# A language-model tower with a routed expert layer on one core: resident experts counted at once, engine orders written anew, and a broadcast product over 128 rows

## The chip, the cores and the metric

The kernel runs on one core of one Trainium2 chip. A core has five engines with a list of instructions each: PE (TensorE, matrix products), DVE (VectorE), ACT (ScalarE), POOL (GpSimd) and SP (SyncE, which here only issues transfers). They meet through semaphores alone. The metric is the device time of one execution in microseconds, as a median of runs.

## The reference

2048 tokens (16 tiles of 128) of width 256 go through two layers. The order of the sums is what matters here:

```python
h = _L0_tok_ref(x, L0_tok_weight)                       # gather of embedding rows
h = h + _L0_attn_ref(_layernorm(h), ...)                # causal linear attention, tile by tile (128 tokens)
h = h + _L0_ffn_ref(_layernorm(h), ...)                 # 256 x 256, scaled weights
h = h + _L1_attn_ref(_layernorm(h), ...)                # random-feature attention, 2-layer FFN
h = h + _L1_ffn_ref(_layernorm(h), ...)                 # router, 8 experts, shared expert

# in _L1_attn_ref, for the keys: the largest feature of a head over all tokens of the sequence
stab = jnp.max(xp, axis=(-1, -2), keepdims=True)
# in _L1_ffn_ref
logits = jnp.einsum('td,ed->te', x, router_w)
top_idx = jnp.argmax(logits, axis=-1)                   # one expert of 8 per token
score = jax.nn.sigmoid(jnp.max(logits, axis=-1))
g = jnp.einsum('td,edf->etf', x * score[:, None], expert_gate)
u = jnp.einsum('td,edf->etf', x * score[:, None], expert_up)
moe_out = jnp.einsum('te,etd->td', onehot, jnp.einsum('etf,efd->etd', silu(g) * u, expert_down))
return moe_out + silu(x @ shared_gate) * (x @ shared_up) @ shared_down
```

## The kernel before

**The token part.** Each of the 16 tiles goes through some 33 stages on PE and as many again on DVE, ACT and POOL: `a_...` is layer 0, `b_...` the attention of layer 1, `c_...` its FFN, the router and the shared expert. The order on an engine is a table of pairs (lag, stage) given to `run_steps`: in step u it runs, in the table's order, each stage for tile u - lag. So several tiles are under way, and the table alone decides what stands behind what. PSUM has 8 banks, which stages share; where two stages of different tiles use one bank, an `after(engine, name, count)` keeps them apart.

Stages that are named below: `b_kq` computes features of keys and queries, `b_km`, `b_kmT`, `kmx`, `b_kmB` find the largest key feature of a head (reduce on DVE, transpose on PE, reduce, and a product with a matrix of ones that gives it to all partitions), `b_qs` subtracts the queries' maxima. `c_T6`, `c_lo`, `c_log`, `c_choose` are the router; `c_cn` is the product that counts a tile's tokens by expert ("count"), `c_slot` turns it into rows of a sorted list, and POOL's `scat` scatters the tokens' numbers there (`sorted_ids`, in DRAM). `c_ga`, `c_up`, `c_dn` are the shared expert's gate, up and down on PE, `c_gc`, `c_hid` (writes `hT`) and `c_down` its parts on DVE. `x_out` and `home_out` on SP store a tile's scaled input and its sum so far to DRAM.

**The tables.** After the last tile's slots DVE computes from the counts which tiles of 128 sorted tokens belong to which expert: `table0` to `table3` for up to 16 whole tiles ("W"), `half_tables` for up to 8 halves of 64 tokens, two to a tile ("H"). `tile_row` and `half_row` give where a tile's ids start in `sorted_ids`; `tile_need` gives how many increments of `experts_ready` a tile's expert needs: max(1, expert - 2).

**The expert part.** 20 tiles in 10 rounds of two (WW, WW, WW, WH, WW, WH, ...; `yA` and `yB` hold the two inputs). POOL fetches their rows of x and of `home` by ids; PE transposes, computes gate and up (`yTA`, `yTB` with `we`), DVE and ACT the gating, PE down (`qkA`, `qkB`), DVE adds `home`, POOL stores to the output. Experts 0 to 3 ("resident", 1.5 MB each) are loaded at the start. Experts 4 to 7 ("late") take the place of the token part's weights, and the H tiles' experts that of `H_S`.

**SP's list at the end** is, in this order: the ids of groups 0 to 3 and the last stores of tiles by `run_steps`; late experts 4 and 5; ids of group 4; late experts 6 and 7; the two experts of the first H tile; ids of group 5; then

```python
            sp.wait_ge(S["residents_loaded"], 16 * RESIDENT)
            sp.sem_inc(S["experts_ready"], 1)
            for e in range(RESIDENT, E):
                sp.wait_ge(late_loaded[e], 16)
                sp.sem_inc(S["experts_ready"], 1)
```

PE waits for a whole tile's `need` of `experts_ready` up to round 5, and for all five later.

## Time and profile before

| | |
|---|---|
| median of 3 runs | 688.7 us (688.22 to 689.7) |
| the profiled execution, its own time | 687.8 us |
| its span, first to last instruction | 686.0 us (1.8 us lie around it) |
| mean granted TensorE clock | 0.973 |
| busy: PE, DVE, ACT, POOL | 619.5, 492.1, 285.8, 254.0 us |
| moved by DMA | 46.85 MB, 68 GB/s on the mean |

Busy shares are means over the whole span; what an engine waits for in one stretch is read from its timeline. A releaser behind an idle time is the instruction whose semaphore came last. A matmul of the code in float32 shows as two records in the trace.

### The profile page before, as it was taken

How to read it: one execution, taken by the hardware profiler on the slowest of the kernel's cores; microseconds unless marked ns; L12 is line 12 of the kernel's file. 1: busy time of each engine (PE TensorE's matmuls, PEld its weight loads, DVE VectorE, ACT ScalarE, POOL GpSimd, SP SyncE). 2: the span in 40 equal slices, each digit the busy share in tenths (PEclk: the TensorE clock that was granted, in tenths of full speed). 3: DMA queues.
4: the chain of work that ended last, by engine and by line, in shares of the span. 5: the costliest groups of instructions: out<-in, count | busy, mean ns of one | idle time of the engine just before them, and what ended most of it. 6: DMA issues, size and time to landing. Idle time of an engine off the chain costs nothing.

```text
span 686.0 us, 15421 instructions
## 1 busy us (share of the span) xinstructions
PE 619.5 (90%) x5960; PEld 500.2 (73%) x5960; DVE 492.1 (72%) x1171; ACT 285.8 (42%) x687; POOL 254.0 (37%) x405
## 2 busy tenths in 40 slices
PE   5878799998999999999999999999993079999997
PEld 4657588887888978898888988989992035555563
DVE  3998999999999988999989988976574012322322
ACT  2345566565465545546454454554320011222221
POOL 5443334435425342442524325312313014435433
PEclk9998999999999999999999999999998579999999
DMA  7950000000000000000000000000012861152550
GB/s 258 415 239 10 1 10 10 1 17 10 10 9 10 24 2 16 10 9 10 10 17 1 17 10 17 10 16 17 16 39 56 324 242 55 61 210 77 226 212 29
DMA packets 17367, 46.85 MB, mean 68 GB/s; under 512 B 6913, under 2 KB 11536, under 8 KB 14864
## 3 DMA queue, kind: packets, MB, share of 16 engines
q1 hardware_dynamic: 13136, 37.47, 14.4%
q0 software_dynamic: 4160, 8.41, 3.9%
q8 instruction: 48, 0.79, 0.7%
q14 instruction: 23, 0.19, 0.2%
HBM read 40.54 MB, written 6.89 MB: 69 GB/s over the span
## 4 chain that ended last, share of the span: by engine, by line
PE 65%; DVE 20%; issue 5%; ACT 3%; SPq 3%; DMA 2%; POOL 0%; another core or an unknown queue 0%; POOLq 0%; DVEq 0%; ACTq 0%
PE ps L1133 61%; DVE stats L716 3%; PE ps L1138 2%; DVE H_S L775 2%; DVE rdenTA L798 1%; SPq L318 1%; PE ps L1290 1%; SPq L317 1%; DVE qf L888 1%; DVE rdenTB L909 1%; ACT qkA L694 1%; DMA home_rows<-send_home 1%; DVE mv L717 1%; DVE x L732 1%; DVE H_S L732 1%
## 5 line engine op out<-in xcount | busy, mean ns | idle before, releaser
L415 POOL TENSOR_TENSOR var_eps<-mv,ln_eps 128x1 f32<-128x1 f32 x112 | 24.3, 217 | 280.2 <-DVE mv L717 275.4
L1133 PE MATMUL ps<-yTC,we 128*128 128x128 f32 x1024 | 123.1, 276 | 0.0
L1133 PEld LDWEIGHTS ps<-yTC,we 128*128 128x128 f32 x1024 | 120.0, 193 | 1.3 <-issue 0.2
L1133 PE MATMUL ps<-we,yTA 128*128 128x256 f32 (+1 forms) x272 | 89.3, 464 | 31.1 <-SPq L376 28.8
L1133 PEld LDWEIGHTS ps<-we,yTA 128*128 128x128 f32 x272 | 50.2, 198 | 52.9 <-issue 49.0
L416 POOL TENSOR_TENSOR rstd<-var_eps,pow_half 128x1 f32<-128x1 f32 x112 | 63.9, 570 | 8.8
L1133 PE MATMUL ps<-we,ffT 128*128 128x256 f32 x256 | 60.8, 380 | 0.0
L1133 PE MATMUL ps<-we,yTB 128*128 128x256 f32 (+1 forms) x176 | 54.8, 440 | 0.0
L1133 PEld LDWEIGHTS ps<-we,ffT 128*128 128x128 f32 x256 | 47.2, 190 | 6.9
L1133 PEld LDWEIGHTS ps<-we,yTB 128*128 128x128 f32 x176 | 32.2, 191 | 13.8 <-issue 11.5
L775 DVE TENSOR_TENSOR H_S<-ps,causal_sb 128x512 f32<-128x512 f32 x64 | 39.9, 677 | 2.0 <-PE ps L1133 2.0
L1114 DVE SCALAR_TENSOR_TENSOR kf<-kf,ps 128x512 f32<-128x512 f32 x10 | 6.9, 688 | 47.7 <-ACT kf L689 47.7
L689 ACT ACTIVATE kf<-ps 128x512 f32<-128x512 f32 x10 | 6.0, 597 | 80.2 <-PE ps L1133 80.2
L909 DVE RECIPROCAL rdenTB<-ps 128x256 f32<-128x256 f32 x16 | 28.1, 1753 | 9.4 <-PE ps L1133 9.4
L1133 PE MATMUL ps<-yTB,we 128*128 128x128 f32 x256 | 32.0, 278 | 2.4 <-ACT yTB L585 2.3
L1133 PEld LDWEIGHTS ps<-yTA,we 128*128 128x128 f32 x256 | 30.2, 192 | 4.4 <-issue 4.2
L1133 PE MATMUL ps<-yTA,we 128*128 128x128 f32 x256 | 32.3, 279 | 0.6 <-ACT yTA L554 0.6
L1133 PEld LDWEIGHTS ps<-yTB,we 128*128 128x128 f32 x256 | 29.8, 192 | 4.1 <-ACT yTB L585 3.5
L1133 PE MATMUL ps<-we,hT 128*128 128x256 f32 x128 | 31.3, 387 | 1.7 <-DVE hT L1082 1.6
L716 DVE BATCH_NORM_STATS2 stats<-H_S 128x6 f32<-128x256 f32 x64 | 27.2, 426 | 5.7 <-DMA H_S<-table,idx_sb 4.1
L625 ACT ACTIVATE kf<-kf 128x1024 f32<-128x1024 f32 x16 | 16.9, 1058 | 34.4 <-DVE kf L897 34.4
L513 POOL DMA_INDIRECT ffT<-home_rows,ids x20 | 20.5, 1024 | 28.7 <-DMA out<-tmpA,ids 15.7
(216 smaller groups left out, 1331.6 us busy)
## 6 DMA issues: line engine op xcount, KB each, us to landing
we<-w_experts SPq DMA_DIRECT2D x8, 1536.0 KB, 13.9
H_S<-w_experts SPq DMA_DIRECT2D x8, 1536.0 KB, 9.7
we<-w_ff SPq DMA_DIRECT2D x2, 1024.0 KB, 9.1
x_rows<-send_x SPq DMA_DIRECT2D x16, 128.0 KB, 1.7
home_rows<-send_home SPq DMA_DIRECT2D x16, 128.0 KB, 2.1
rows_sb<-rows SPq DMA_DIRECT2D x1, 1664.0 KB, 6.3
we<-w_qk SPq DMA_DIRECT2D x2, 512.0 KB, 4.5
we<-w_v SPq DMA_DIRECT2D x2, 256.0 KB, 4.7
```

The lines of the kernel that those rows point to most:

```text
L317: first = sp.value_load(table_of[0:1, k:k + 1], min_val=0, max_val=E * SPAN * P)
L415: link(pool.tensor_tensor(var_eps[:, k:k + 1], mv[:, k, 1:2], ln_eps[:], ALU.add))
L416: pool.tensor_tensor(rstd[:, k:k + 1], var_eps[:, k:k + 1], pow_half[:], ALU.pow).then_inc(S[f"rstd{k}_ready"], 1)
L513: pool.indirect_dma_start(out=home[s], out_offset=None, in_=home_rows, in_offset=by_id(j), bounds_check=T * P - 1, oob_is_err=False).then_ ...
L625: act.activation(flat(kf[:]), flat(kf[:]), ACT.Exp).then_inc(S["kexp_out"], 1)
L716: link(dve.bn_stats(stats[:, k], src))
L732: return dve.scalar_tensor_tensor(out=dst, in0=buf, scalar=rstd[:, k:k + 1], in1=rest, op0=ALU.mult, op1=ALU.add)
L775: dve.tensor_tensor(S_sb[:, b], by4(sc[b]), causal_sb[:].unsqueeze(1).broadcast_to([P, 4, P]), ALU.mult).then_inc(S["scores_masked"], 1)
L909: dve.reciprocal(rdenTB[:], nd1[:, D:2 * D]).then_inc(S["rden1_ready"], 1)
L1114: dve.scalar_tensor_tensor(out=eg2[s], in0=eg1[s], scalar=1.0, in1=banks_of[s][1], op0=ALU.add, op1=ALU.mult).then_inc(S["eg_ready"], 1)
L1133: return pe.matmul(o, a, b, start=start, stop=stop)
L1138: ins = pe.transpose(dst[:, c * P:(c + 1) * P], src[:, c * P:(c + 1) * P], id_sb[:])
```

## The change

Four things are changed, and no amount of work but for the broadcast.

1. SP's `ids0` increments `experts_ready` for the residents before it reads the first ids. The late experts are counted as soon as they are there: 4 and 5 ahead of the first halves' loads, 6 and 7 ahead of the ids of group 5.
2. The five tables of `run_steps` are new, and with them the PSUM banks of the stages and the `after` waits that they need. DVE's `b_norm` now waits for the `preB` of the tile before, and POOL's `pB` for `var4` of the tile before. On PE gate and up move from lags 9 and 10 to 11 and 11, down from 11 to 12.
3. SP reads ids of group 1 right behind group 0 and one store, group 2 and 3 behind the last stores.
4. `b_kmB` is a product with all 128 rows (`one_all`, `km_diag` of 128 partitions, of which 16 are written), where it had 16.

```diff
-        km_diag = sb("km_diag", [HEADS, HEADS])
-        one16 = sb("one16", [HEADS, P])
+        km_diag = sb("km_diag", [P, HEADS])
+        one_all = sb("one_all", [P, P])
...
                 if t == T - 1:
+                    sp.wait_ge(S["residents_loaded"], 16 * RESIDENT)
+                    sp.sem_inc(S["experts_ready"], 1)
                     sp.wait_ge(S["table_ready"], 1)
                     sp.wait_ge(S["ids_scattered"], 16 * T)
                     load_ids(0)
...
             run_steps([
-                (1, ids0), (10, ids3), (4, ids1), (0, x_out), (8, ids2), (2, home_out),
+                (1, ids0), (5, ids3), (0, x_out), (3, home_out), (1, ids1), (4, ids2),
             ])
...
+            def late_is_ready(e):
+                sp.wait_ge(late_loaded[e], 16)
+                sp.sem_inc(S["experts_ready"], 1)
+
             load_late(RESIDENT)
             load_late(RESIDENT + 1)
             load_ids(4)
             load_late(RESIDENT + 2)
             load_late(RESIDENT + 3)
...
+            late_is_ready(RESIDENT)
+            late_is_ready(RESIDENT + 1)
             sp.wait_ge(S["tile_done"], T)
             sp.wait_ge(S["table_ready"], 2)
             load_halves(0)
+            late_is_ready(RESIDENT + 2)
+            late_is_ready(RESIDENT + 3)
             load_ids(5)
-            sp.wait_ge(S["residents_loaded"], 16 * RESIDENT)
-            sp.sem_inc(S["experts_ready"], 1)
-            for e in range(RESIDENT, E):
-                sp.wait_ge(late_loaded[e], 16)
-                sp.sem_inc(S["experts_ready"], 1)
...
                 pool.wait_ge(S["src3_ready"], t + 1)
+                after(pool, "var4_ready", t)
                 pool.tensor_tensor(preB[:], yB[:], row["out1_bias"], ALU.add).then_inc(S["preB_ready"], 1)
...
             def b_norm(t):
-
+                after(dve, "preB_ready", t)
                 normalise(yB[:], H[:, t, :], 3, t).then_inc(S["src3_ready"], 1)
...
-                matmul(kb[:, 0:HEADS], one16[:], km_diag[:], True, True).then_inc(S["kmax_psum"], 1)
+                matmul(kb[:, 0:HEADS], one_all[:], km_diag[:], True, True).then_inc(S["kmax_psum"], 1)
...
-                (9, c_ga), (0, a_v), (7, c_lo), (5, c_T5), (1, a_num), (4, b_ctx),
+                (1, a_den), (4, b_v), (6, c_fa), (11, c_up), (5, b_out), (8, c_cn),
```

On PE, from the last tile's count to the first expert tile's transposes, there stood before (`yTC` of number k with `we` is gate or up of tile 12 + k, `hT` is down, `yA` the first expert tile's input):

```order
L1133 MATMUL ps<-onehot,ones_sb 128x8
L1133 MATMUL ps<-yTC_2,we 128x128 x8
L1133 MATMUL ps<-we,hT 128x256 x4
L1133 MATMUL ps<-yTC_2,we 128x128 x8
L1133 MATMUL ps<-yTC_3,we 128x128 x8
L1133 MATMUL ps<-we,hT 128x256 x4
L1133 MATMUL ps<-yTC_3,we 128x128 x8
L1133 MATMUL ps<-we,hT 128x256 x4
L1408 MATMUL ps<-id_sb,yA 128x128 x2
```

In the changed kernel the same stretch of PE's list reads:

```order
L1138 MATMUL ps<-onehot,ones_sb 128x8
L1138 MATMUL ps<-yTC_1,we 128x128 x8
L1138 MATMUL ps<-we,hT 128x256 x4
L1138 MATMUL ps<-yTC_1,we 128x128 x8
L1138 MATMUL ps<-yTC_2,we 128x128 x8
L1138 MATMUL ps<-we,hT 128x256 x4
L1138 MATMUL ps<-yTC_2,we 128x128 x8
L1138 MATMUL ps<-yTC_3,we 128x128 x8
L1138 MATMUL ps<-we,hT 128x256 x4
L1138 MATMUL ps<-yTC_3,we 128x128 x8
L1138 MATMUL ps<-we,hT 128x256 x4
L1418 MATMUL ps<-id_sb,yA 128x128 x2
```

Seven groups stood behind the last count, ten do now: one gate, one up and one down have moved behind it. On SP, at the reading of the first ids, this is the difference (`tile_row` loads an address, `ids` is the transfer, `home_rows` a tile's store):

```order
-L302 DMA x_rows<-send_x 128x256 [waits sent_ready]
+L317 TENSOR_LOAD tile_row [waits residents_loaded,table_ready,ids_scattered]
+L317 ISA x2
+L318 REGISTER_ALU
+L318 DMA ids<-sorted_ids 128x1
+L317 TENSOR_LOAD tile_row
+L317 ISA x2
+L318 REGISTER_ALU
+L318 DMA ids<-sorted_ids 128x1
 L307 DMA home_rows<-send_home 128x256 [waits tile_done]
```

The ids of group 0 now stand ahead of one more store of a tile, and the last three stores come behind them. Further down SP's list, behind the second pair of late experts, the changed kernel has:

```order
L351 DMA we<-w_experts 128x3072 x2
L361 TENSOR_LOAD half_expert [waits late_loaded4,late_loaded5,tile_done,table_ready]
L361 ISA x2
L362 ISA
L362 DMA H_S<-w_experts 128x3072
L361 TENSOR_LOAD half_expert
L361 ISA x2
L362 ISA
L362 DMA H_S<-w_experts 128x3072
L317 TENSOR_LOAD tile_row [waits late_loaded6,late_loaded7]
```

There the waits for the late experts now stand among the loads; before, they stood behind the ids of group 5.

## Rows read from the trace of the kernel before

**Rows 1.** The page's section 2, granted TensorE clock in 40 slices (tenths)

```profile
PEclk9998999999999999999999999999998579999999
```

**Rows 2.** Four stretches by windows; busy us of each engine, PEclk, DMA share, GB/s

```profile
0.00:506.40 506.40, 480.57 (x5368) 418.70 (x5369) 442.29 (x1058) 254.35 (x625) 192.25 (x344) 0.99 0.12 41
506.40:524.85 18.45, 13.99 (x95) 12.20 (x93) 12.12 (x45) 1.58 (x3) 3.02 (x3) 1.00 0.16 48
524.85:553.66 28.81, 0.00 (x1) 0.01 (x1) 1.79 (x9) 0.38 (x1) 3.99 (x4) 0.53 0.73 279
553.66:686.00 132.34, 124.97 (x500) 69.30 (x500) 35.94 (x60) 29.47 (x58) 54.77 (x54) 0.99 0.36 128
```

**Rows 3.** Timeline of PE, 500 to 554 us; start, duration, idle before and releaser

```profile
506.38 0.17 PE L1133 MATMUL ps<-onehot,ones_sb 128*128 128x8 f16 x1
...
519.23 1.99 PE L1133 MATMUL ps<-we,hT 128*128 128x256 f32 x8 [1.55 <-DVE hT L1082]
523.16 0.41 PE L1408 MATMUL ps<-id_sb,yA 128*128 128x128 f32 x2 [1.94 <-DMA yA<-x_rows,ids]
524.41 0.44 PE L1408 MATMUL ps<-id_sb,yB 128*128 128x128 f32 x2 [0.84 <-DMA yB<-x_rows,ids]
553.66 5.52 PE L1133 MATMUL ps<-we,yTA 128*128 x8 [28.81 <-SPq L376]
```

**Rows 4.** Timeline of SP's queue, 515 to 554 us

```profile
515.66 2.02 SPq L318 DMA_DIRECT2D ids<-sorted_ids  x2
...
522.86 10.12 SPq L318 DMA_DIRECT2D ids<-sorted_ids  x9
533.24 0.81 SPq L349 DMA_DIRECT2D we<-w_experts  x2
...
540.03 0.91 SPq L349 DMA_DIRECT2D we<-w_experts  x2
...
544.51 8.83 SPq L318 DMA_DIRECT2D ids<-sorted_ids  x8
```

**Rows 5.** Issue to landing of line 349: experts 4 and 5, then 6 and 7

```profile
DMA to landing us min/median/max: 6.4/8.1/9.7
DMA to landing us min/median/max: 8.7/10.3/11.9
```

**Rows 6.** Windows of 2 us in the loads of the late experts

```profile
548.00:550.00 2.00, 0.00 (x0) 0.00 (x0) 0.00 (x0) 0.00 (x0) 0.00 (x0) 0.50 1.02 430
```

**Rows 7.** Timeline of PE, rounds 1 and 2 of the expert part

```profile
568.10 3.70 PE L1133 MATMUL ps<-we,yTA 128*128 x8
...
580.73 3.69 PE L1133 MATMUL ps<-we,yTA 128*128 x8
584.26 3.60 PE L1133 MATMUL ps<-we,yTB 128*128 x8
```

**Rows 8.** A load by tile, a group of the page, an add by line

```profile
L1133 PEld LDWEIGHTS ps<-km_diag,one x32: 181/184/328, 54.9 to 459.8; 16*128 16x128 f32 x32
...
L1133 PEld LDWEIGHTS ps<-yTC,we 128*128 128x128 f32 x1024 | 120.0, 193 | 1.3 <-issue 0.2
...
L469 POOL TENSOR_TENSOR preB<-yB,rows_sb x16: 720/774/1747, 47.0 to 460.6; 128x256 f32<-128x256 f32 x16
```

**Rows 9.** Timeline of POOL, the last scatter

```profile
507.82 0.96 POOL L486 DMA_INDIRECT sorted_ids<-tokens,slot_u  x1 [5.11 <-DVE slot_u L981]
```

**Rows 10.** Windows of the steps that start at tiles 9 and 10

```profile
188.58:217.88 29.30, 28.70 (x332) 25.11 (x331) 28.26 (x71) 16.16 (x41) 11.98 (x22) 1.00 0.03 10
217.88:248.26 30.38, 30.17 (x341) 26.61 (x339) 28.31 (x68) 15.78 (x40) 12.78 (x23) 1.00 0.07 15
```

**Rows 11.** Issue to landing: stores under loads, stores otherwise, ids at 544 us

```profile
DMA to landing us min/median/max: 7.2/7.2/7.3
...
DMA to landing us min/median/max: 2.4/2.5/2.5
...
DMA to landing us min/median/max: 8.5/11.1/14.6
```

More of the change, by code:

```diff
@@ L1100, in _ @@
             run_steps([
[L1101 to L1105 removed]
+                (2, a_m0), (2, a_m2), (9, c_log), (3, a_res), (10, table2), (0, a_stats), (5, b_dgr), (1, a_max),
+                (6, b_cx), (11, table3), (5, b_qs), (6, b_rec), (9, c_choose), (5, b_vo), (6, b_mean), (5, b_km),
+                (3, a_norm2), (8, c_res), (12, c_hid), (6, b_o), (8, c_norm), (9, c_slot), (1, a_elu), (5, kmx),
+                (9, table0), (4, b_norm), (2, a_rec), (6, b_x1), (5, b_ks), (11, c_gc), (2, a_mean), (0, a_norm),
+                (7, c_o), (1, a_vz), (3, a_ff), (9, table1), (2, a_o), (1, a_m1), (1, a_m3), (12, c_down),
             ])
```

117 lines of the change are left out of this document (58 added, 59 removed).

## The prediction

> **What bounds the kernel now.** I read the page's slices first: the granted TensorE clock is at full speed but for three slices of 8, 5 and 7 tenths, three quarters of the way through [rows 1]. The windows put borders on it: up to 506.4 us PE is busy 480.6 of 506.4 us; then comes a hand-over of 18.45 us; then 28.81 us in which PE does nothing at all while the DMA moves 279 GB/s; then the experts, 132.3 us with PE busy 125.0 [rows 2]. So there are three things to watch: a token part that PE bounds, a hole, an expert part that PE bounds.
>
> The timeline of PE names the hole: the inputs of the first two expert tiles are transposed at 523.16 and 524.41, and the first product with an expert starts at 553.66 after 28.81 us released by SP's line 376 [rows 3]. That line is in the run of increments of `experts_ready` at the end of SP's list, and the first of them (line 373) is all that a tile of a resident expert needs. The residents are loaded at the very start of the run, so PE waits only for SP to get to the increment: SP issues 9 loads of ids from 522.86, late experts 4 and 5 at 533.24, 5 ids, experts 6 and 7 at 540.03, the two halves, and 8 more ids from 544.51 that take it to 553.3 [rows 4].
>
> **What the change does there.** `ids0` increments `experts_ready` before the first ids are read, so the hole's cause goes. What comes next depends on which experts the first tiles have. Evaluating the reference's router on its inputs gives 1, 3, 633, 21, 14, 33, 9 and 1334 tokens for experts 0 to 7. By `table0` a whole tile is placed for each multiple of 128 that a count exceeds by more than 64: five for expert 2 (resident), ten for expert 7. Whole tiles 0 to 4 are expert 2's and tile 5, the second of round 2, is expert 7's and needs `experts_ready` at 5: all four late loads. Rounds 0, 1 and half of 2 can run at once; then expert 7 is what is late next.
>
> Its time follows from SP. In the kernel before, the last product of the token part ended at 519.23 + 1.99 = 521.22 [rows 3] and the late loads started at 533.24, 12.0 later; between them lie the half tables on DVE (they can't start before the last `c_down`), and five ids at about 1.15 us each. The change leaves this alone (the ids of group 1 leave this stretch, but group 3 waits for the tables anyway), so I keep 12.0. Experts 4 and 5 landed 6.4 and 9.7 us after their issue, 6 and 7 in 8.7 and 11.9 [rows 5]; the longest, for expert 7, is counted from its own issue at 540.5, so it landed at 552.4, 19.2 behind the start of the late loads. Now two rounds run beside the loads: two stores and two fetches of `home`, 0.13 MB each, at the 430 GB/s of the loads' windows [rows 6] add 1.2 us. Expert 7 is there 12.0 + 19.2 + 1.2 = 32.4 us after the token part's last product. The new waits on experts 4 and 5 hold SP for some 2 us, until 10.1 us behind the start of the loads [rows 4, 5]. Behind them in its queue are the halves, the increments and the ids of group 5; the halves are queued behind expert 7 in both kernels and needed in round 3 only, so this costs nothing.
>
> PE gets to tile 5 earlier: 0.9 us for transposes and ACT's copy, two rounds of 12.63 us and one tile of 3.53 [rows 7] make 29.7 us. So PE waits 2.7 us for expert 7. From tile 5's product to the end the kernel before took 686.0 - 584.26 = 101.7 us; I keep it. Halves and later ids land well before round 3.
>
> **The order of the token part.** The sum of PE's work is the same: one broadcast product has 128 rows where it had 16. Its weight load took 184 ns at 16 rows, and a load of 128 rows and 128 columns took 193 [rows 8]: 9 ns over 32 loads are 0.3 us as an upper bound, and I take 0. A longer memset and a new one stand at the start, beside the gathers that DVE waits for: 0.
>
> What moves is where work stands. Behind the last count product PE had seven groups of 8 or 4 matmuls (about 1.86 us each) and now ten (the pieces of PE's order in the section on the change). The chain that runs beside them: last count at 506.38, scatter issued at 507.82, ids read from 515.66, inputs there at 523.16 and 524.41 [rows 3, 4, 9], that is 16.8 and 18.0 us behind the count. Seven groups left PE idle for it; ten take 18.6 us plus about 0.8 for the last `hT`, so the token part ends 19.4 us after the count and x is not waited for any more. That is worth 1 us there. SP sits in the scatter's wait with `home_out` of tiles 13 to 15 behind it; `c_down` of tile 14 waits for tile 13's store to be issued at count + 11.4 and landed at 13.5, and it is not due before its product ends at 15.0. Hidden, by 1.5 us.
>
> The three groups were done before the count until now, so the count comes up to 5.6 us earlier, if the steps that lose them get shorter. Gate, up and down start one or two steps later, so 7.4 us of PE leaves steps 9 to 11. There DVE is busy 28.26 of 29.30 and 28.31 of 30.38 us [rows 10]: it is nearly full itself, and the move takes only about 1.8 us (and a residual, 1.3) off it. Bounds: nothing lost, the part ends at 506.4 - 5.6 + 19.4 = 520.2; only 1.8 of 7.4 kept, 525.8. I take about the middle, a loss of 2.7: **522.9**.
>
> Sum: 522.9 + 32.4 + 101.7 = 657.0 us of span, and 1.8 around it: **658.8 us** against the profiled run's 687.8. The median shown, 688.7, stands 0.9 above that run, so I say 659. The same from the other side: the first expert product starts at 523.8, not 553.66 (-29.9); the first round took 14.44 with a PE clock that the hole had taken to half [rows 2, 7] and takes 12.63 now (-1.8); expert 7 gives 2.7 back.
>
> **A rule weighed.** A store of the expert part took 7.2 us to land when two half experts were loading, against 2.5 otherwise, while ids queued on SP's own queue behind loads took 8.5 to 14.6 [rows 11]. The chain that this could bring to the front is store of round 0, fetch of `home`, fetch of x for round 3, all in POOL's order. The store is issued at 537 (the first round's end and DVE's add), lands at 544.2, the two fetches of `home` and then of x are issued by 550 at 1.3 us each, and land by 557; PE wants them after tile 5's products, at 522.9 + 32.4 + 3.6 = 558.9: hidden by 2 us. The Trainium skill (DMA: Bandwidth & Descriptors, Queues, rings and completion order) says that each DMA engine takes turns between its queues packet by packet; POOL's small transfers would then share and not queue, which is the 7.2. By the middle one of SP's own landings, 11.1, the two legs would be 4 us longer each and the sum about 6 us higher.
>
> **The rivals.** *Experts in time* (0.15): the token part ends late or the loads go faster, PE never waits, and the end is 29.7 + 101.7 behind its last product: from 520.2, 653.4. For it: only 2.7 us separate the two. *The order costs more* (0.17): the new order lets PE run dry while the pipeline fills. DVE now does `b_qs`, four passes over 128x512, ahead of `b_km`, for which PE's first step of the features waits; in the kernel before, DVE's busy share leaves it a microsecond or two a step [rows 10]. With one to two us more lost in each of steps 5 to 8, 663 to 668. *Fetches starve* (0.06): 665. *Nothing released* (0.03): if tile 0 were an expert 7 tile, PE would wait as before: about 685. *Slower* (0.04): `b_norm` waits for `preB` of the tile before, and that POOL step now waits for `var4`: a round trip DVE, POOL, DVE in every one of 16 steps. The add alone takes 0.77 us [rows 8] and stands in a row of POOL waits; it decides if it costs over 29 / 16 = 1.8 us a step; at 2.5, 699 us. Against it: DVE has nine other instructions between (`c_norm`, `c_slot`, `a_elu`, `kmx`). The forecast itself keeps 0.55.
>
> A clock drop in the 2.7 us wait would cost at most the 5.52 - 3.70 = 1.8 us of the first tile after the hole [rows 3, 7]; it is in the range. Low end: a token part 1.4 us shorter than its lower bound and no wait, 518.8 + 29.7 + 101.7 + 1.8 = 652. High end: 525.8 + 32.4 + 1.8 + 101.7 + 1.8 = 663.5, plus half of what starving fetches cost: 667. Less than 0.2% either way this measurement can't tell from no change: faster 0.95, same 0.01, slower 0.04.
>
> **What would show it.** Right: PE's first expert product within 2 us of the second transpose, released by ACT; a wait of 1 to 5 us before `yTB` of round 2, released by SP's line in `late_is_ready`; the clock at full up to there; last count near 503.5, last `hT` product ending near 523. Wrong: the wait at round 0 stays; PE idle in steps 5 to 8 grows by over 5 us; DVE waits on POOL's `preB` in every step; round 3 waits for x.

## The result and the profile after

The changed kernel takes **679.9 us** (median of 4, 678.6 to 681.9) against 689.2 (median of 4, 688.2 to 692.0) for the kernel before beside it: ratio 0.986, interval 0.982 to 0.990. Forecast were 659 us, 652 to 667. The direction was right; less than a third of the gain came. The profiled execution took 681.9 us, its span is 680.1.

The windows of the changed kernel have the borders of [rows 2]: last count, end of the token part, first product with an expert (columns as there):

```profile
0.00:525.37 525.37, 486.86 (x5327) 426.31 (x5328) 449.07 (x1056) 254.85 (x624) 184.77 (x344) 0.98 0.11 40
525.37:545.56 20.19, 18.69 (x134) 17.24 (x132) 10.76 (x33) 1.79 (x3) 3.02 (x3) 1.00 0.15 40
545.56:547.40 1.84, 0.44 (x6) 0.21 (x3) 1.63 (x7) 0.66 (x2) 0.79 (x1) 1.00 0.21 71
547.40:680.00 132.60, 123.42 (x500) 68.51 (x500) 39.48 (x77) 29.47 (x58) 58.01 (x58) 1.00 0.51 189
```

The hole of 28.81 us is gone, and the experts take the same 132 to 133 us. But the first window is 19.0 us longer: PE is idle for 12.7 us more of it, and busy for 6.3 us more although three groups of 1.86 us have left it. The timeline of PE at the hand-over answers to [rows 3] and [rows 7]:

```profile
525.37 0.17 PE L1138 MATMUL ps<-onehot,ones_sb 128*128 128x8 f16 x1
...
543.57 1.99 PE L1138 MATMUL ps<-we,hT 128*128 128x256 f32 x8 [0.85 <-DVE hT L1086]
545.40 0.38 PE L1418 MATMUL ps<-id_sb,yA 128*128 128x128 f32 x2
...
547.40 3.69 PE L1138 MATMUL ps<-we,yTA 128*128 x8 [1.40 <-ACT yTB L689]
...
578.17 2.41 PE L1138 MATMUL ps<-we,yTB 128*128 x5 [1.82 <-SPq L366]
```

The first product waits 1.40 us for ACT, no longer for SP; `yTB` of round 2 waits 1.82 us for line 366, which is in `late_is_ready`. SP's queue, to be held against [rows 4]:

```profile
535.62 2.04 SPq L318 DMA_DIRECT2D ids<-sorted_ids  x2
...
558.50 0.23 SPq L351 DMA_DIRECT2D we<-w_experts  x2
...
564.81 0.92 SPq L351 DMA_DIRECT2D we<-w_experts  x2
```

The late loads start 12.9 us behind the token part's end. Nearly everything about the hole is as forecast. What is not is the token part, so the following goes by the start of `a_T0` of a tile on PE ("T0(4)" is tile 4's):

| us | kernel before | forecast | after |
|---|---|---|---|
| T0(4) starts | 41.5 | 41.5 | 53.5 |
| from there to the last count | 464.9 | 462.0 | 471.9 |
| last count to the end of the token part | 14.8 | 19.4 | 20.2 |
| token part ends | 521.2 | 522.9 | 545.6 |

Of the 22.7 us that the forecast misses, 12.0 are there by T0(4), 9.9 come behind it, and 0.8 behind the count. But T0(4) is not quite the same point in both kernels. The new table puts `a_T2` and `a_ffn` of tile 1, `b_qk` of tile 0 and `a_out` of tile 2 in front of it, and the old one has them behind it: 26 records, 4.6 us of PE. Up to T0(4) PE is busy 40.2 us where it was 30.4, and idle 13.3 where it was 11.1. So of the 12.0 us some 4.6 are these four stages, some 5 are slower products, and 2.2 are more waiting. The timeline of PE in the first steps of the changed kernel:

```profile
10.37 3.43 PE L1138 MATMUL ps<-yTA,we 128*128 128x128 f32 x16 [0.63 <-ACT yTA L559]
...
16.83 0.44 PE L1143 MATMUL ps<-id_sb,yA 128*128 128x128 f32 x2 [1.93 <-DVE yA L726]
17.49 2.08 PE L1138 MATMUL ps<-qz,qkA 32*128 32x256 f32 x16 [0.22 <-ACT qz L577]
...
27.55 1.88 PE L1138 MATMUL ps<-we,yTA 128*128 128x256 f32 x4 [2.30 <-DVE yTA L807]
29.22 0.63 PE L1143 MATMUL ps<-id_sb,yA 128*128 128x128 f32 x2
```

The product at 27.55 is `a_out` of tile 0. It waits for DVE's `yTA`, and T0(2) stands behind it: 29.22 where the kernel before had 21.86. The products at 10.37 and 17.49 take 3.43 and 2.08 us; the same ones took 2.02 and 1.15 there. The page's slices of the granted clock ([rows 1]) say why:

```profile
PEclk8799989999999999899999999999999999999999
```

The first slices are 8 and 7 tenths: the granted clock is at its lower level, 0.5, in three stretches before T0(4), 10.2 us in all, and in the kernel before in none. Later, from step 11 on, waits appear that no semaphore explains ("issue"), in the middle of a run of short products:

```profile
270.58 0.60 PE L1138 MATMUL ps<-qfT,ctxbd 128*32 128x128 f32 x10
273.56 1.35 PE L1138 MATMUL ps<-qfT,ctxbd 128*32 128x128 f32 x19 [2.38 <-issue]
...
371.19 0.64 PE L1138 MATMUL ps<-H_S,den_oneA 128*32 128x256 f32 x3 [1.76 <-issue]
```

They sum to 8.5 us between 130 us and the end of the token part; the kernel before has none there. Behind those of 2.38 and 1.76 us the granted clock falls to 0.5 as well (from 273.6 and from 372.5 us), which costs 1.7 us each time. From T0(12) to the last count both kernels have the same 2724 records of PE. The windows of that stretch, before and after:

```profile
248.26:506.38 258.12, 255.89 (x2724) 229.34 (x2723) 218.41 (x543) 127.15 (x315) 87.44 (x154) 1.00 0.05 13
```

```profile
259.41:525.37 265.96, 256.23 (x2724) 231.28 (x2723) 217.75 (x542) 125.88 (x311) 86.69 (x157) 0.99 0.05 13
```

PE is idle 9.7 us there and was idle 2.2; 7.8 of the 9.7 are waits without a releaser.

DVE has the same instructions in both kernels, but for one memset of 0.07 us, and yet is busy 500.9 us where it was 492.1; 6.8 of these 8.8 us lie ahead of the last count. Single instructions have got longer. `km_diag` took 221 to 224 ns in each of the 16 steps before; now it takes 344 in the median, and three times 1.5 us. One of these, with POOL and PE beside it:

```profile
193.58 1.54 DVE L869 TENSOR_SCALAR km_diag<-id_sb,km_head 16x16 f32<-16x16 f32 x1
193.66 0.74 POOL L484 TENSOR_TENSOR H_S<-H_S,rows_sb 128x256 f32<-128x256 f32 x1
194.35 0.73 POOL L463 TENSOR_TENSOR preA<-H_S,rows_sb 128x256 f32<-128x256 f32 x1
195.17 0.40 PE L1138 MATMUL ps<-km_diag,one_all 128*128 128x16 f32 x2 [1.43 <-DVE km_diag L869]
```

It ends when POOL's second operation ends, and PE waits 1.43 us for it. The instructions that grew most are `qmax<-qmax,diag` (8.6 us in all for 2.8), `km_diag` (9.0 for 3.6) and `yC` (11.9 for 7.6). Wherever they are long POOL has an operation beside them; in the kernel before it had none beside the first two. Two others (`x`, `tmpC`) were long beside POOL before and have got shorter. No run sets this apart from the rest of the new order.

Last, the windows from T0(10) to T0(11) and from there to T0(12), which answer to [rows 10]:

```profile
201.23:229.36 28.13, 26.82 (x316) 23.62 (x315) 27.16 (x64) 15.66 (x39) 11.06 (x21) 1.00 0.04 11
229.36:259.41 30.05, 29.17 (x332) 25.46 (x331) 28.46 (x66) 15.66 (x39) 11.06 (x21) 1.00 0.04 11
```

With 1.9 and 1.0 us less work for PE the steps are 1.2 and 0.3 us shorter (the two before them are 1.2 and 0.5 longer), and DVE is busy 27.2 of 28.1: the first is as long as DVE's work.

### The profile page after: what moved, and what is told of

It is laid out like the page before. It is cut to its first block, busy times and chain, and to the rows that moved or that the text cites. A ratio compares the mean times of both kernels' runs of the same rounds, so it can differ in the third digit from the quotient of the medians.

```text
span 680.1 us, 15388 instructions
## 1 busy us (share of the span) xinstructions
PE 629.4 (93%) x5960; PEld 512.3 (75%) x5960; DVE 500.9 (74%) x1172; ACT 286.8 (42%) x687; POOL 246.6 (36%) x405
## 4 chain that ended last, share of the span: by engine, by line
PE 51%; DVE 32%; issue 8%; DMA 4%; ACT 2%; SPq 1%; another core or an unknown queue 0%; POOL 0%; POOLq 0%; DVEq 0%; ACTq 0%
PE ps L1138 48%; DVE H_S L779 4%; DVE stats L721 4%; DVE rdenTB L913 2%; PE ps L1143 2%; DMA we<-w_experts 2%; DVE rdenTA L802 2%; DVE qf L892 2%; DVE qkA L766 2%; DVE mv L722 1%; DVE kmax L863 1%; DVE H_S L737 1%; DVE yC L726 1%; DMA home_rows<-send_home 1%; PE ps L1291 1%
## 5 line engine op out<-in xcount | busy, mean ns | idle before, releaser
L1138 PEld LDWEIGHTS ps<-yTC,we 128*128 128x128 f32 x1024 | 121.9, 194 | 2.0 <-issue 0.2
L1138 PE MATMUL ps<-we,yTB 128*128 128x256 f32 (+1 forms) x176 | 57.3, 454 | 4.7 <-DVE yTB L918 2.8
L1138 PEld LDWEIGHTS ps<-yTA,we 128*128 128x128 f32 x256 | 31.8, 202 | 6.2 <-issue 5.8
L1138 PE MATMUL ps<-yTA,we 128*128 128x128 f32 x256 | 34.9, 293 | 0.6 <-ACT yTA L559 0.6
L650 ACT ACTIVATE ffT<-ps,cols_sb 128x128 f32<-128x128 f32 x64 | 18.3, 370 | 37.4 <-PE ps L1138 37.4
L1128 DVE TENSOR_TENSOR tmpA<-ps,ffT 128x256 f32<-128x256 f32 x10 | 4.3, 425 | 36.8 <-DMA ffT<-home_rows,ids 19.4
L638 ACT ACTIVATE qfT<-ps 128x1024 f32<-128x1024 f32 x16 | 16.4, 1026 | 31.4 <-PE ps L1291 31.4
```

Of the source, the lines that this page charges most:

```text
L638: act.activation(flat(qfT[:]), flat(qT), ACT.Copy, bias=EPS_K).then_inc(S["qT_ready"], 1)
L650: act.activation(ffT[:, f, :], fa[:, f * P:f * P + P], ACT.Relu, bias=b1_col[:, f:f + 1]).then_inc(S["ffa_ready"], 1)
L1138: return pe.matmul(o, a, b, start=start, stop=stop)
```

## The experiments

Each ratio is to the kernel before on the same chip, whose median lay between 689.2 and 693.6 us. "Issue" is the sum of PE's waits without a releaser between 130 us and the last count, in us.

| kernel | ratio, interval | T0(4) | last count | issue |
|---|---|---|---|---|
| changed | 0.986, 0.982 to 0.990 | 53.5 | 525.4 | 8.5 |
| e8 changed, again | 0.986, 0.982 to 0.989 | 51.8 | 517.5 | 7.4 |
| e1 old order, early count | 0.961, 0.959 to 0.964 | 43.1 | 509.1 | 0.3 |
| e2 new order, late count | 1.030, 1.026 to 1.033 | 53.3 | 529.5 | 12.9 |
| e3 old, broadcast | 0.996, 0.994 to 0.998 | 43.2 | 507.9 | 0.3 |
| e7 old order, early count, broadcast | 0.958, 0.955 to 0.961 | 43.1 | 504.6 | 0.3 |
| e4 changed, fill | 1.004, 1.001 to 1.007 | 62.4 | 537.9 | 12.5 |
| e13 changed, loop open | 0.993, 0.990 to 0.996 | 59.4 | 529.0 | 11.5 |
| e5 changed, warm | 0.975, 0.970 to 0.980 | 49.1 | 512.8 | 4.9 |
| e6 changed, `b_h` apart | 1.042, 1.038 to 1.045 | 51.6 | 561.6 | 9.0 |
| e10 changed, light statistics | 0.978, 0.974 to 0.982 | 53.3 | 519.4 | 11.1 |
| e11 changed, a step earlier | 0.978, 0.975 to 0.981 | 49.1 | 512.9 | 6.1 |
| e12 changed, short twice | 0.993, 0.990 to 0.996 | 52.1 | 526.5 | 10.2 |
| e15 e13 and e11 | 0.991, 0.988 to 0.995 | 58.7 | 531.4 | 5.9 |
| e9 e7, warm | 0.966, 0.963 to 0.969 | 43.8 | 514.1 | 0.3 |
| e14 e7, 14 more at the start | 0.963, 0.960 to 0.966 | 42.0 | 505.0 | 0.3 |
| e16 e7, `a_out` ahead | 0.973, 0.969 to 0.977 | 53.6 | 516.4 | 0.3 |
| e17 e7, short twice | 0.981, 0.978 to 0.984 | 45.0 | 522.4 | 6.2 |
| e18 e7, warm hand-over | 0.954, 0.951 to 0.957 | 43.7 | 508.0 | 0.3 |

### Which part of the change gives, which takes: e1, e2, e3, e7

e1 is the kernel before with SP's list alone changed:

```diff
                 if t == T - 1:
+                    sp.wait_ge(S["residents_loaded"], 16 * RESIDENT)
+                    sp.sem_inc(S["experts_ready"], 1)
                     sp.wait_ge(S["table_ready"], 1)
```

with `late_is_ready` as in the change. Expected: 

> The kernel before, with SP's list alone changed: the increment for the residents in ids0, the late experts counted as they come. Orders, banks and broadcast as before. Theory (the order of the token part is what cost, the early count gave what was forecast): the token part stays (last count at 506.4, last hT product ends at 521.2), PE's first expert product at about 526 instead of 553.7, expert 7 there 32.4 us behind the token part, and the end 101.7 behind that: 656 to 660 us. Rival (the early count itself costs in the token part or in the experts what the changed kernel lost): 675 to 680.

Measured 0.961, 666.6 us on a slower chip; 0.961 of 689.2 is 662.4, still 2.4 above the band. The last count stands at 509.1 and not at 506.4; T0(4) is 1.6 us late already, with a stretch of the lower clock from 16 us on that the kernel before doesn't have. The theory's point holds all the same: the early count alone gives 27 us, nearly three times what the whole change gives.

e2 puts the increments back behind the ids of group 5. Expected: 

> The changed kernel with the increments put back behind the ids of group 5 in SP's list; orders, banks, waits and broadcast are the changed kernel's. Theory (hole and order are separate sums): token part ends at 545.6 as in the changed kernel, SP reaches the increment some 33 us later, at 579, and the experts take 132.3 from there: 711 us (706 to 715). Rival (the order costs only where the experts start early): near the kernel before, 689 to 695.

Measured 1.030; 715.2 us beside 693.6, which is 709.7 of 689.2. The new order, with the broadcast in it, makes the kernel 3% slower when it has no early count to pay for it, and the two sums are separate.

e3 is the broadcast alone (`one_all`, `km_diag` of 128 partitions). Expected: 

> The kernel before with the broadcast product over all 128 rows and nothing else. Theory: the weight loads and the product do not grow by anything that can be measured: 688 to 690 us, km_diag's operation on DVE stays at 221 ns. Rival (the 128-row tile is what made DVE's km_diag operation take 563 ns in the changed kernel, 0.34 us in each of 16 steps, with the wait of PE on it): 693 to 696.

Measured 0.996: faster by 3 us, which neither theory had. The view of the tile `km_diag` shows where. It gives the loads of weights (PEld) and the idle time ahead of them, first with 16 rows (e1), then with 128 (e3):

```profile
L1137 PEld LDWEIGHTS ps<-km_diag,one x32: 181/184/328, 56.5 to 462.5; 16*128 16x128 f32 x32
  issue: 6.8, 14
```

```profile
L1134 PEld LDWEIGHTS ps<-km_diag,one_all x32: 186/190/337, 56.6 to 460.4; 128*128 128x128 f32 x32
  issue: 2.5, 1
```

The load is as long, but 13 of the 16-row loads start 0.33 us behind the end of the load before them, with no releaser; of the 128-row ones none does (one pause of 2.5 us is in both). These are pauses between loads: PE's products themselves have hardly any idle time without a releaser (0.3 us in all in e1). What the kernel gets is that the product behind the broadcast starts 1.28 us behind the start of the product before it with 16 rows and 1.00 with 128 (at 126 us in both runs). DVE's `km_diag` operation keeps its 222 ns in e3, so its 344 ns (median) in the changed kernel are not the broadcast's.

e7 has both parts that gained, in the old order. Expected: 

> The kernel before with SP's list changed as in the first experiment and the broadcast over all 128 rows, with the old orders: the two parts of the change that gained, without the part that lost. If they add up (ratios 0.9611 and 0.9957): 0.957 of the kernel before, 659.5 us on the chip of the first runs; PE's waits of about 0.5 us ahead of the broadcast product that no semaphore explains (12 of them, 6.0 us) are gone. Rival (the 3 us of the broadcast were chance, or lie beside the hole): the ratio of the first experiment, 0.961.

Measured 0.958, 660.6 us, as if they add. What the expectation calls PE's waits are the pauses of its loads. Its interval overlaps e1's, so that it is faster than e1 by itself isn't shown.

### The measure again: e8

> The changed kernel itself once more, as the measure for the other three on the same chip: 0.986 of the kernel before; its waits of PE that no semaphore explains stand at the same instructions again, 8.5 us in all between tile 3 and the end of the token part.

The same program gave 0.986 again, with its issue waits at the same instructions, give or take a few records. In the profiles one execution stands 7.9 us ahead of the other at the last count (517.5, 525.4), and 1.7 of them by T0(4). The clock makes most of it: up to the last count it is at 0.5 for seven stretches in the first execution and for three in this one, and each costs 1.7 us. So the 9.9 us behind T0(4) are one execution's; here the way from T0(4) to the last count is 465.7 us, 3.7 above the forecast. A difference between two profiles is read below only where their clocks have been compared, or where it is much larger than this.

### The first steps: e4, e13, e5, e16

e4 moves `a_norm` of tiles 1 to 3 ahead on DVE and `a_out` of tiles 0 to 2 behind `a_T0` and `a_qk` on PE:

```diff
             def a_max(t):
+                if t < FILL:
+                    a_norm(t + 1, early=True)
...
+                if 2 <= t < FILL + 2:          # at the end of PE's a_qk
+                    a_out(t - 2, moved=True)
```

Expected: 

> The changed kernel, but in the first steps DVE normalises tiles 1, 2 and 3 ahead of a_max of the tile before (PE's a_T0 then waits for x_ready of the tile before, since both use one bank), and PE runs a_out of tiles 0 to 2 behind a_T0 and a_qk of two tiles later. The steps behind them are those of the changed kernel. Theory (11 of the 19 us that the last count is late are lost before 41 us, because PE stands behind DVE's order while the pipeline fills): T0 of tile 4 starts 4 to 8 us earlier than 53.5, and the time falls by as much: 672 to 676 us. Rival (the steps behind them are bound by something else that takes the lead back): within 1 us of 679.9.

A miss, and the wrong way: 1.004. The timeline of DVE says what became of it:

```profile
33.21 0.42 DVE L817 TENSOR_TENSOR tmpA<-ps,rows_sb 128x256 f32<-128x256 f32 x1 [4.18 <-PE ps L1143]
```

DVE's `a_o` waits 4.18 us for `a_out`, and the masks of the next tile, which PE's `a_num` needs, are behind it (PE waits 4.22 us for them). The lateness of 8.9 to 10.6 us at T0(4) against the changed kernel is still there at the last count (12.5 and 20.4): what the first steps lose is not made up.

e13 moves DVE's `a_o` behind those masks as well. Expected: 

> As the fourth experiment (which was slower: DVE waited 4.2 us a step for a_out's product with the next tile's masks queued behind it), with one edit more: for tiles 0 to 2 DVE runs a_o behind the four masks of the tile after, not ahead of them. Theory (in the new order the first steps are a serial loop, one tile each time: scores, masks, num and den, reciprocal, yTA, a_out, and only behind it on PE the next tile's transposes and scores; 12 us a step at T0 of tiles 2 to 4 against 8 in the old order): with a_out out of the loop on both engines the steps of tiles 1 to 3 take 8 to 10 us, T0 of tile 4 starts at 44 to 48 us instead of 51.8 to 53.5, and the whole time falls by 4 to 8 us against the changed kernel: ratio to the kernel before 0.974 to 0.980. Rival (the first steps were late by the clock or by loads): T0 of tile 4 stays over 50.

A miss again, T0(4) at 59.4. T0(2) came at 26.5, where it was 27.3 and 29.2, and then PE stood 4.27 us ahead of `a_T2` of tile 0, which stands ahead of T0(3) in the new table: behind one link of the loop lies the next.

e5 leaves the order alone and fills PE's waits with products of ones (8, 6, 20 and 24 of them). Expected: 

> The changed kernel with products of ones added on PE: 8 more at the start, 6 ahead of the first a_qk, 20 ahead of a_T0 of tile 1, 24 ahead of a_out of tile 0 (all into a bank that nothing uses yet, some 0.09 us each). They fill PE's waits of 0.6, 1.9 and 2.3 us in the first steps and change no order. Theory (of the 11 us lost before 41 us some 4 are products at the half clock: 3.43 for 2.02, 2.08 for 1.15, 2.74 for 2.05, 1.82 for 1.15 us; the rest is waiting): these products take their full-clock durations and the time falls by 2 to 4 us against the changed kernel of the same batch. Rival (the waits grow by what the products give up, since the chain through DVE and ACT is what lasts): within 1 us, or slower by the added products, up to 3 us.

0.975, some 7 us below the changed kernel, more than expected. The products take their full-clock times (2.02, 1.15, 2.05), and T0(4) starts at 49.1. So of the 12.0 us about 4.4 are clock. Of the 7.6 that are left, 4.6 are the four stages that now stand ahead of T0(4), and 3.0 are waiting.

e16 goes the other way: one link of the new order put into e7.

```diff
             def a_T0(t):
+                if 2 <= t < FILL + 2:          # FILL = 2
+                    a_out(t - 2, moved=True)
                 pe.wait_ge(S["src0_ready"], t + 1)
```

Expected: 

> The kernel of old orders, early count and 128-row broadcast (0.958), with one link of the new order put into its first steps: PE runs a_out of tiles 0 and 1 ahead of a_T0 of tiles 2 and 3, as the changed kernel does. Nothing else moves. Theory (that link makes the next tile's transposes and scores wait for the reciprocal and yTA of the tile before, which is what makes the first steps of the new order 12 us long): T0 of tile 2 starts 2 to 3 us later than 23.4, T0 of tile 4 3 to 6 us later than 43.1, and the lateness stays to the end: 0.962 to 0.967. Rival (the link is harmless by itself, other parts of the new order do it): T0 of tile 4 within 1 us of 43.1, 0.958.

The link costs, and more than the theory said. PE's timeline in e7, then in e16:

```profile
22.45 1.05 PE L1138 MATMUL ps<-H_S,den_oneA 128*32 128x256 f32 x16
23.43 0.44 PE L1143 MATMUL ps<-id_sb,yA 128*128 128x128 f32 x2
```

```profile
25.21 2.08 PE L1140 MATMUL ps<-we,yTA 128*128 128x256 f32 x4 [2.74 <-DVE yTA L809]
27.08 0.63 PE L1145 MATMUL ps<-id_sb,yA 128*128 128x128 f32 x2
...
41.51 2.07 PE L1140 MATMUL ps<-we,yTA 128*128 128x256 f32 x4 [6.24 <-DVE yTA L809]
43.37 0.64 PE L1145 MATMUL ps<-id_sb,yA 128*128 128x128 f32 x2
```

`a_out` waits 2.74 and 6.24 us and takes 2.08 us at the lower clock; T0(4) comes 10.5 us later, with the same work ahead of it, the last count 11.8, and the ratio is 0.973 for 0.958, some 10 us. About 3 of the 10.5 are clock: products at the lower level last 4.7 us longer in e16 before T0(4), and 1.6 in e7. Two groups of products of 1 us each, put ahead of the next tile's transposes, cost the whole kernel ten. The size is that of DVE's old order, which has the reciprocal a step later: in the changed kernel `a_out` waits 2.30 and 0.61 us at the same places.

### The steps in the middle: e10, e11

e10 takes the statistics of all norms over 128 of the 256 columns. Expected: 

> The changed kernel with the statistics of all norms over 128 of the 256 columns (part of the computation is left out: mean and variance come from half the row). It takes some 0.14 us from each of seven operations, 1.0 us of DVE a step, and touches nothing on PE. Theory (in steps 7 to 10 DVE is the bound: 27.2 of 28.1 us busy, so the 7.4 us of gate, up and down that the new order takes away from PE there could not shorten them): each of the steps 5 to 11 gets 0.7 to 1.2 us shorter, the last count comes 5 to 9 us earlier than 517 to 525. Rival (waits on single results and on issue set those steps): steps 5 to 11 shorten by less than 2 us in all.

The windows from T0(5) to T0(12), e8 and then e10 (columns as in [rows 2]):

```profile
69.75:256.10 186.35, 173.94 (x2066) 150.29 (x2064) 178.39 (x400) 102.84 (x251) 73.71 (x134) 0.99 0.04 10
```

```profile
72.13:253.66 181.53, 171.27 (x2066) 148.97 (x2065) 172.21 (x399) 102.57 (x250) 73.29 (x134) 1.00 0.04 10
```

6.2 us less of DVE's work made the seven steps 4.8 us shorter, with the same matmuls: far above the rival's 2 (the theory gave 0.7 to 1.2 a step), and DVE is busy 96 and 95% of them. PE is busy 2.7 us less in e10, which is clock (0.99 against 1.00), but that isn't the gain: e4 has the changed kernel's order in these seven steps, a clock of 1.00 and 171.6 us of PE, and takes 186.9 us. The last count doesn't come earlier for it (466.1 us behind T0(4), 465.7 in e8), against the theory's 5 to 9: issue waits of 11.1 us, two of them 3.6 and 3.9 long, ate the gain later. The time is 5 us less than the changed kernel's.

e11 undoes one step of the deferral on all engines.

```diff
-                (9, table1) ... (11, c_ga) ... (11, c_up) ... (12, c_dn)
+                (9, table1) ... (10, c_ga) ... (10, c_up) ... (11, c_dn)
```

Expected: 

> The changed kernel with gate, up and down on all engines one step earlier (PE lags 10, 10, 11; the waits that keep banks apart moved with them). Half of what the change moved is moved back: four groups fewer behind the last count, 7.4 us of PE back into steps 10 and 11. Forecast of the prediction's step (PE bounds there, so the deferral shortens the steps before the count): last count 4 to 7 us later than in the changed kernel. Theory now (DVE bounds steps 7 to 10, the deferral gains nothing there, and behind the count x is waited for anyway): last count at most 2 us later, the count to the first expert product 17 to 21.4 us, time within 3 us of the changed kernel's.

Behind the last count seven groups stand again, as in the kernel before, so three have moved back ahead of it. The forecast's step would have the way from T0(4) to the last count 4 to 7 us longer; it is 463.8 us against 465.7 in e8 and 463.7 in e5, whose clock is as high, and the ratio is 0.978 against 0.986, more than the 3 us that the theory allowed. So by the last count the deferral of that step had gained nothing. In its own three steps, from T0(9) to T0(12), it had: they take 88.5 us in e11, 85.7 in e8, 86.3 in the changed kernel. What e11 pays there it has back by the last count, where its waits are fewer.

### The waits without a releaser: e6, e12, e17, e9, e14

e6 moves `b_h` behind `a_den`, `b_v` and `c_fa` on PE. Expected: 

> The changed kernel, but PE runs b_h (32 products of 32 columns) behind a_den, b_v and c_fa, not between a_num and a_den; b_v waits for ctx_even and ctx_odd of the tile before, as b_h did, since it shares the bank. Theory (the waits of 2.38, 1.76, 1.13 and 0.24 us that no semaphore explains stand where b_ctx, b_kq, a_num, b_h and a_den put 144 short products into 9 us, and come from PE running out of issued instructions there): they vanish, and with them 4 to 7 us of the time against the changed kernel of the same batch. Rival (they come from something else, such as a transfer or the clock; or b_h's later end makes DVE late): the waits stay or wander, time within 1 us or slower.

1.042. The edit made its own wait, by PE's list of waits:

```profile
PE ps L1138 <- DVE yTB L918: 24.5, 14, 3.3
PE ps L1138 <- issue: 9.0, 16, 2.1
```

`b_out` now waits for what DVE makes of `b_h`, in 14 steps. The issue waits did not vanish but moved to `a_den` and to the long products of `c_fa`. That the place of one group makes them is not borne out.

e12 issues `a_num` twice. Expected: 

> The changed kernel with a_num issued twice in a row (the second writes the same numbers again): 32 more short records in each step, 0.9 us of PE at full clock, 14.4 us in all, between a_num and b_h where the waits without a semaphore stand. Theory (PE runs out of issued instructions where short products crowd): these waits grow from the 7.4 to 8.5 us of the changed kernel to over 15 us between tile 3 and the end of the token part, and the time by 14 to 25 us. Rival (they are tied to something else): they stay under 9 us and the time grows by 5 to 14 us, by what DVE's slack hides.

10.2 us for 7.4 to 8.5, and 5 us on the time: between the two, nearer the rival. In the new order this doesn't tell.

e17 does the same in e7, which has 0.3 us of such waits. Expected: 

> The same kernel as the measure, with a_num issued twice in a row (the same numbers written again): 112 short records stand together ahead of b_T3, 0.9 us more a step, 14.4 us in all. In the changed kernel the same edit cost 5 us and its waits without a semaphore went only from 7.4 to 10.2 us. Theory (crowded short products run PE out of issued instructions): such waits, absent in the old order between tile 3 and the last count, appear, 2 us or more in all, and the time is 0.975 to 0.985. Rival (crowding is not what makes them): none appear, the time grows by the 10 to 14 us of the added products or what waits hide of them.

```profile
226.28 0.59 PE L1138 MATMUL ps<-H_S,den_oneA 128*32 128x256 f32 x1 [3.65 <-issue]
...
354.25 0.78 PE L1138 MATMUL ps<-H_S,den_oneA 128*32 128x256 f32 x4 [1.96 <-issue]
```

Now they are there, 6.2 us in four, the long ones at the end of the crowd of 112, and the ratio of 0.981 is the theory's. The edit also shifts the program, but e9, e14 and e18 below shift the same program without a crowd and keep their 0.3 us. So crowded short products do bring them; but not in every step, only in two or three of sixteen, and why there is open.

e9 and e14 shift the program of e7. e9 adds products of ones in the first steps. Expected: 

> The kernel of old orders, early count and 128-row broadcast (0.958 of the kernel before), with 8 more products of ones at the start, 6 ahead of the first a_qk and 20 ahead of the first a_s. Theory (in the changed kernel such products gave 6 us, since the clock stayed up in the first steps; here the first steps show slices of 9, 8 and 7 tenths too): T0 of tile 2 back from 23.4 to about 21.9, time 1.5 to 3 us less: 0.954 to 0.956. Rival (the waits there are longer than the products fill, the clock falls anyway): 0.958.

T0(2) came back to 22.5, yet the ratio is 0.966 for 0.958, in five executions within 0.9 us of each other. The loss is on another engine, in ACT's timeline (`remote` is a releaser to which the view gives no name), and the DMA view of 218 to 226 us shows what moved then:

```profile
219.83 0.37 ACT L581 ACTIVATE denA<-ps 128x256 f32<-128x256 f32 x1
224.48 0.38 ACT L589 ACTIVATE yTB<-ps 128x256 f32<-128x256 f32 x1 [4.28 <-remote]
```

```profile
q8 instruction: 1, 0.02, 2.9%
q14 instruction: 1, 0.01, 2.4%
```

ACT waits 4.28 us for a value that had been there (in e7 it goes on at 219.12), PE 3.82 us for ACT, and the clock falls to 0.5 behind it. A second such wait, 2.79 us of PE at 348 us, ends the same way; the two waits with their clock sum to some 10 us, and the last count is 9.5 us later than in e7. The only transfers beside the first wait are two of the queues of kind instruction. The Trainium skill (Runtime: NRT & Kernel Launch, Instruction fetch mechanics) says that a sequencer refills its instruction memory in blocks of 16 KiB over a DMA queue of its own, and that this is mostly hidden. The trace agrees on the block for q8 (48 packets, 0.79 MB, in most runs); q14's packets are of 8 KB. That such a refill is what ACT waited for is not shown: e7 has the same two packets between 218 and 226 us and no wait, and beside PE's wait of 2.38 us in the changed kernel (270 to 274 us) no such packet moves.

e14 adds 14 products at the very start. Expected: 

> The kernel of old orders, early count and 128-row broadcast (0.958) with 14 more products of ones at the start and nothing else: 0.9 us of PE work that lies in the wait for the first input. It differs from the run that took 0.966 in the 20 products ahead of the first a_s. Theory (that run lost 10 us in two waits for ACT of 3.8 and 2.8 us and a few like them, which come from where the program of an engine stands when its next piece of code has to come, and so from any shift of the sequence): the time is anywhere from 0.955 to 0.970, and its waits stand at other instructions than in either. Rival (the 20 products themselves cost it): 0.958 as without, within 0.2%.

0.963, between the two, with an interval that touches both, and a profile as e7's (last count 505.0), taken of its fastest execution. So this one shift of the program costs half a per cent if anything. Whether the 20 products ahead of the first `a_s` make the rest of e9's 0.8%, or the place to which they bring ACT, is open.

### What can be taken back: e15, e18

e15 joins e13 and e11. Expected: 

> The edits of the two experiments that took something back from the new order together: the loop of the first steps opened, and gate, up and down one step earlier. If they add: 4 to 8 us and 5 us below the changed kernel, ratio 0.967 to 0.973. It then still lies above the old order's 0.958 by what the waits without a semaphore cost in steps 12 to 15 (some 4 us) and the rest of the first steps.

0.991: nothing adds, as e13 by itself had lost, and e11's 0.8% doesn't show on top of e13's 0.993.

e18 is e7 with products of ones at the hand-over. Expected: 

> The same kernel as the measure, with 24 and 14 products of ones ahead of the two transposes of the first expert tiles' inputs and 16 behind them, in a bank that nothing uses then (where PE waits 1.7, 1.1 and 2.5 us). The token part's program does not shift. Theory (the first product with an expert takes 5.2 instead of 3.7 us because PE's clock fell in these waits): it takes 3.7 to 4.2 us and the time is 1 to 1.5 us less, 0.956. Rival (the products delay the register loads behind them, or the clock stays down): 0.958 or up to 0.2% above.

The first expert product in e7 and in e18:

```profile
525.64 5.22 PE L1138 MATMUL ps<-we,yTA 128*128 x8 [2.51 <-issue]
```

```profile
530.43 3.70 PE L1138 MATMUL ps<-we,yTA 128*128 x8 [1.81 <-issue]
```

It takes 3.70 for 5.22 us, and the ratio is 0.954, the lowest of all; its interval (0.951 to 0.957) still touches e7's (0.955 to 0.961).

## Why the prediction was wrong

**The hole and what follows: right.** Forecast and measured: PE waits for ACT at the first product, yes; late loads 12.0 / 12.9 us behind the token part; tile 5's product 32.4 / 32.6 behind it; PE's wait there 2.7 / 1.8; from there to the end 101.7 / 101.9; around the span 1.8 / 1.8. Nothing starved, no clock fell behind the token part. e1 has this part of the change alone.

**The step that failed: the order of the token part.** The prediction wrote "PE's work is the same", and so looked only for what leaves steps 9 to 11: 5.6 us to gain, "I take about the middle, a loss of 2.7". The token part ended at 545.6, not 522.9, and outside even its bound of 525.8. Three terms are missing or wrong.

- *The first steps had no term: 12.0 us by T0(4).* 4.6 of them are only stages that now stand ahead of T0(4), 4.4 are clock that fell in the waits (e5), and 3.0 are waiting. The first steps hold one chain, not a full engine: scores, masks, `a_num` and `a_den`, reciprocal, `yTA`, `a_out`. The old lags (`a_rec` 3, `a_o` 4) spread it over two steps, and PE has the next tile's transposes and scores in front of `a_out`; the new ones (2 and 2) close it, with `a_out` in front. e16 shows that this link alone can cost 10.5 us at T0(4), in DVE's old order and with some 3 us of clock. That it is what the changed kernel's waits come from is argued from its rows; e4 and e13, meant to open it there, closed it elsewhere.
- *The deferral's 2.9 us did not come.* From T0(9) to T0(12) the changed kernel takes 86.3 us (85.7 in e8) for 87.4, and e7, with the broadcast and without the deferral, 85.8. The prediction had DVE at 28.3 of 29.3 us in its own rows and bounded the gain by "only 1.8 of 7.4 kept". The bound had to be DVE's work, and "PE's work is the same" says nothing of that: in the new order DVE's same instructions take 8.8 us longer, and PE waits for some of them. e10 shows that these steps follow DVE's work, e11 that moving the three groups back costs 2.2 to 2.8 us in these steps and nothing by the last count. What the 8.8 us cost was not tried.
- *Waits without a releaser had no term: 7.9 us from T0(12) to the last count, 3.3 in e8.* PE's records are the same 2724 as before, and 7.8 of its 9.7 us of idle time are such waits, which also take the clock down twice. e17 shows that crowding brings such waits; that crowding makes all of them here was not shown. Two other waits on the way, 3.1 us of `a_v` on the new wait for `counts_read` and 3.8 of the 4.0 on `km_diag`, lie in the steps before T0(12); the kernel before waits 3.7 us on `km_diag` too, in its first two steps with that stage.

Behind the count the forecast held (19.4 / 20.2), but was worth less than the 1 us given to it: from the last count to the first product with an expert it takes 22.0 us in the changed kernel (21.5 in e8) and 21.1 in e7, where x is waited for. What three groups more fill there, the old order spends waiting.

**The broadcast: wrong by 3 us.** Only the load was priced; its own row said 0. The pause ahead of a load with fewer rows had no row in the prediction, though the trace of before has it (6.0 us in 12 pauses of PEld).

**A reading.** The prediction names three slices of the clock below full. The row has a fourth, the 8 in the fourth slice (the clock is at 0.5 from 52 to 59 us), while the pipeline fills: it was the sign that waits there cost clock as well.

**The rivals.** *The order costs more* (0.17, 663 to 668) was the nearest by its kind, "lets PE run dry while the pipeline fills". It was placed in steps 5 to 8, at one to two us each. There the changed kernel lost 1.7 us in all: from T0(5) to T0(9) it takes 100.1 us, and the kernel before 98.4. Most of the loss stands in the first steps and from step 12 on. *Slower* by the round trip of `preB` had its wait, but nobody behind it, by POOL's group:

```profile
L474 POOL TENSOR_TENSOR preB<-yB,rows_sb 128x256 f32<-128x256 f32 x16 | 15.2, 947 | 23.4 <-DVE mv L722 23.4
```

23.4 us of POOL's time, and no row in which DVE waits for it. *Experts in time* is what e7 does: PE waits for no expert, and behind the first round of 14.2 us the next takes 12.6.

## What to carry to other kernels

When a table of lags is changed, walk one tile's chain through it for the first steps, where nothing else fills the engines: a lag taken out or a consumer put in front of the next tile's first stage can close a loop there, and what was lost so was still there at the end (e16: 10.5 us, then 11.8). When two orders are compared at a marker such as T0(4), count what each has in front of it first. An engine's work moved away from a step shortens it only down to the next engine's work, so the bound is that engine's busy time, not a share of the gain; and that busy time is the new order's, not the old one's. And run the parts of a change by themselves: here two small ones gave 4.2%, and the large one took two thirds of it back.

## What the runs showed of the hardware that was not expected

- The weight load of a float32 product with 16 rows, among loads of 128 rows, started 0.33 us behind the end of the load before it, without a releaser, 13 times of 16; with 128 rows (zeros but for 16) never. Worth 0.4% (e3).
- The same DVE instruction can last longer by what POOL does beside it: `km_diag` 1.54 us for 0.22, to the end of POOL's second operation, and PE waits 1.43 us for it. A new order of the same instructions made DVE's work 8.8 us longer (500.9, and 499.9 in e8, for 492.1).
- An engine can wait 1 to 4 us with no semaphore outstanding. On PE it came where over 100 short records stand together (e17: 3.65 us), on ACT at single instructions (e9: 4.28 us), at nearly the same place in two executions of a program (e8). In the changed kernel the clock fell to 0.5 behind two such waits, of 2.38 and 1.76 us, and cost 1.7 us more each time; in e8 it didn't behind one of 1.77.
- 34 products of some 0.09 us, all but hidden, made a kernel 0.8% slower (e9), 14 of them 0.5% at the edge of the intervals (e14), and 58 in another order 1.0% faster (e5). Differences of half a per cent may come from where a program's instructions stand; no run here sets that apart from everything else.
